# Attention: third score unit behind the mix, next batch's normalising on ScalarE, three engines' orders changed

## The reference

```
xn = (x - mean(x)) / sqrt(var(x) + 1e-5)
q, k, v = xn @ Wq + bq, xn @ Wk + bk, xn @ Wv + bv      # 16 heads of 64
q, k = rope(q), rope(k)
p = softmax(causal(q @ k.T / 8))
x = x + (p @ v) @ Wo + bo
```

## Time and profile before

| | us |
|---|---|
| median of 3 runs | 2759.45 |
| profiled execution | 2767.62 |
| its span | 2765.8 |
| PE busy | 2537.4 (92%) |
| PEld busy | 1909.4 (69%) |
| DVE busy | 1835.4 (66%) |
| ACT busy | 1512.0 (55%) |
| POOL busy | 1462.2 (53%) |

### The profile page before, as it was taken

How to read it: one execution, slowest core, us unless ns; L and a number is a source line. 1 busy time by engine, 2 the same in 40 slices (tenths; PEclk the granted TensorE clock), 3 DMA queues, 4 the chain that set the end, 5 groups by cost and what they waited for, 6 DMA issues and landing times. The chain is left out here.

```text
span 2765.8 us, 53186 instructions
## 1 busy us (share of the span) xinstructions
PE 2537.4 (92%) x16856; PEld 1909.4 (69%) x16856; DVE 1835.4 (66%) x3300; ACT 1512.0 (55%) x3793; POOL 1462.2 (53%) x1264
## 2 busy tenths in 40 slices
PE   7986998899999999999999998999999997986899
PEld 5752676677777777777777776777777774753576
DVE  6741576677777776677767776777677775751376
ACT  2321443666666667666676666766767662321343
POOL 1100543767667677676676766767767661100343
PEclk9997999999999999999999999999999999998999
DMA  7459553323333333233333332323333326359543
GB/s 239 161 226 401 188 156 116 69 58 82 67 71 86 63 71 74 67 84 65 74 81 60 83 65 66 88 64 73 71 71 83 66 63 203 122 203 412 178 151 104
DMA packets 252348, 326.69 MB, mean 118 GB/s; under 512 B 60704, under 2 KB 205728, under 8 KB 247968
## 3 DMA queue, kind: packets, MB, share of 16 engines
q1 hardware_dynamic: 252064, 323.24, 41.5%
HBM read 211.98 MB, written 44.04 MB: 93 GB/s over the span
## 5 line engine op out<-in xcount | busy, mean ns | idle before, releaser
L1524 ACT ACTIVATE att_prob<-att_ps_s,att_nmax 128x512 f32<-128x512 f32 (+3 forms) x1024 | 529.2, 526 | 375.3 <-DVE att_nmax L1426 364.0
L1327 POOL TENSOR_TENSOR att_z_sb<-att_z_sb,sh_vT 128x512 f32<-128x512 f32 x255 | 331.0, 1298 | 381.0 <-DMA att_zs<-att_z_sb 380.9
L1652 PE MATMUL att_ps_p<-sh_ident,att_prob 128*128 128x128 f32 x2560 | 405.5, 282 | 77.9 <-DVE att_probT L1440 76.2
L1426 DVE TENSOR_REDUCE att_nmax<-att_ps_s 128x2 f32<-128x1024 f32 (+3 forms) x512 | 410.2, 822 | 13.3
L1652 PEld LDWEIGHTS att_ps_p<-sh_ident,att_prob 128*128 128x128 f32 x2560 | 296.0, 142 | 132.8 <-DVE att_probT L1440 97.4
L1330 POOL TENSOR_TENSOR att_z_sb<-att_z_sb,att_zs 128x512 f32<-128x512 f32 x255 | 347.0, 1361 | 20.0
L1452 DVE TENSOR_TENSOR att_oT_lo<-sh_kT,att_oT_hi 128x512 fp32r<-128x512 f32 x128 | 158.2, 1236 | 292.0 <-ACT att_oT_hi L1544 292.0
L1328 POOL TENSOR_TENSOR att_zs<-att_zs,att_sin 128x512 f32<-128x512 f32 x255 | 338.0, 1326 | 0.0
L1663 PE MATMUL att_ps_p<-att_probT,att_v_sb 128*64 128x512 f32 (+3 forms) x2048 | 307.1, 442 | 3.7 <-ACT att_probT L1539 2.4
L1539 ACT COPY att_probT<-att_ps_p 128x512 f32<-128x512 f32 x384 | 215.9, 600 | 135.1 <-PE att_ps_p L1652 134.8
L1663 PEld LDWEIGHTS att_ps_p<-att_probT,att_v_sb 128*64 128x64 f32 x2048 | 138.4, 137 | 176.6 <-issue 131.3
(11 more groups left out here) (198 smaller groups left out, 5715.8 us busy)
## 6 DMA issues: line engine op xcount, KB each, us to landing
att_zs<-att_z_sb SPq DMA_DIRECT2D x1024, 64.0 KB, 2.3
ffn_w<-in_e_W SPq DMA_DIRECT2D x56, 1024.0 KB, 13.7
att_R<-inverse_sums SPq DMA_DIRECT2D x256, 128.0 KB, 3.3
ffn_wg<-in_e_Wg SPq DMA_DIRECT2D x24, 1024.0 KB, 14.3
x_normalised_transposed<-dis_b_xnT SPq DMA_DIRECT2D x32, 512.0 KB, 2.7
dis_b_x<-in_x SPq DMA_DIRECT2D x16, 512.0 KB, 4.3
ex_w<-in_e_W SPq DMA_DIRECT2D x8, 1024.0 KB, 12.3
ex_wg<-in_e_Wg SPq DMA_DIRECT2D x8, 1024.0 KB, 15.7
```

The costliest lines, as they stand in the source:

```text
L1327: nc.gpsimd.tensor_tensor(z[:, m, i, :], z[:, m, i, :], cos[:], ALU.mult)
L1426: nc.vector.tensor_reduce(nmax[:, p % 2, qt, :], ps[:, :, at:at + (qt + 1) * P], AX.X, ALU.max, negate=True)\
L1524: nc.scalar.activation(prob[:, p % 2, hh, PLACE[qt]], ps[:, hh, at:at + (qt + 1) * P], ACT.Exp, bias=nmax[:, p % 2, qt, hh:hh + 1], accum_ ...
L1652: last = nc.tensor.transpose(turn_bank(k)[:, at:at + P], prob[:, p % 2, hh, PLACE[qt]][:, kb * P:(kb + 1) * P], g.ident[:])
```

## The change

TensorE: `scores(j, p, 2)` moves from behind the first half of the values to right behind the mix, ahead of both projections. VectorE: the third `largest` moves ahead of `low_part` and the first copy, all four statistics go behind the query's low part, and `normalise` is gone; one small instruction `recentre` makes -mean * rstd. ScalarE: `normalise` is four activations with a scale and a bias for each partition, behind the query copy; `high_part` goes ahead of the evacuations, and the exponentials of tiles 1 and 0 go up, tile 1 between the evacuation of the queries and that of the keys. GpSimd: the rstd of the next batch are made in slot 5 between the rotation of the keys and that of the queries, instead of at the end of slot 4. The code of SP is not changed.

```diff
@@ gpsimd, slot
                     rotate(j, p + 1, 1)
+                    if p == X_TURN and not t.last:
+                        layernorm_rstd(nc, g, pool, mv, veps, rstd, TT, mom_s, veps_s, rstd_s, j + 1)
...
-                if p == X_LOAD and not t.last:
-                    layernorm_rstd(nc, g, pool, mv, veps, rstd, TT, mom_s, veps_s, rstd_s, j + 1)
@@ vector
-            def normalise(j):
+            def recentre(j):
                 dve.wait_ge(rstd_s.sem, rstd_s.at(j, 1))
-                for i in range(TT):
-                    nc.vector.scalar_tensor_tensor(xin[:, i, :], xin[:, i, :], mv[:, i, 0:1], rstd[:, i:i + 1].broadcast_to([P, D]),
-                                                   ALU.subtract, ALU.mult).then_inc(xn_s.sem, 1)
+                nc.vector.scalar_tensor_tensor(shift[:], mv[:, :, 0], -1.0, rstd[:], ALU.mult, ALU.mult).then_inc(stats_s.sem, 1)
@@ vector, slot
-                if loading:
-                    statistics(j + 1, (0, 1))
...
-                if loading:
-                    statistics(j + 1, (2, 3))
+                if p == X_LOAD and not t.last:
+                    statistics(j + 1, range(TT))
                     moments(j + 1)
@@ scalar
+            def normalise(j):
+                act.wait_ge(stats_s.sem, stats_s.at(j, TT + 1))
+                for i in range(TT):
+                    nc.scalar.activation(xin[:, i, :], xin[:, i, :], ACT.Identity, bias=shift[:, i:i + 1], scale=rstd[:, i:i + 1]).then_inc(xn_s.sem, 1)
@@ scalar, slot
                     exps(j, p, 3)
-                if t.has(p):
                     exps(j, p, 2)
+                if t.has(p - 2):
+                    high_part(j, p - 2)
                 if t.has(p + 2):
                     evacuate(j, p + 2, 0)
+                if t.has(p):
+                    exps(j, p, 1)
+                if t.has(p + 2):
                     evacuate(j, p + 2, 1)
@@ tensor, slot
                     mix(j, p - 2)
+                if t.has(p):
+                    scores(j, p, 2)
                 if t.has(p + 2):
                     project(t, p + 2, 0)
```

More of the change, by code:

```diff
@@ L1169, in attention_phase @@
     x_in, xres_in, out_s = c("x_in", 16), c("xres_in", 16), c("out", 16, 16)
-    stats_s, mom_s, veps_s, rstd_s, xn_s = c("stats", TT), c("moments", TT), c("veps", 1), c("rstd", 1), c("xn", TT)
+    stats_s, mom_s, veps_s, rstd_s, xn_s = c("stats", TT + 1, -1), c("moments", TT), c("veps", 1), c("rstd", 1), c("xn", TT)
     xt_mm, xhi_s, xlo_s = c("xt_mm", DC), c("xhi", DC), c("xlo", DC)
@@ L1236, in attention_phase @@
         acc, xout = (sb(x, [P, TT, D]) for x in ("acc", "xout"))
-        stats, mv, veps, rstd = sb("st", [P, TT, 6]), sb("mv", [P, TT, 2]), sb("ve", [P, TT]), sb("rs", [P, TT])
+        stats, mv, veps, rstd, shift = sb("st", [P, TT, 6]), sb("mv", [P, TT, 2]), sb("ve", [P, TT]), sb("rs", [P, TT]), sb("shift", [P, TT])
         xT = g.xT
@@ L1456, in slot @@
                 j, p = t.j, t.p
-                loading, turning = p == X_LOAD and not t.last, p == X_TURN and not t.last
                 if p == X_TURN + 1 and not t.last:
@@ L1467, in slot @@
                     divide(j, p - 2)
-                if turning:
-                    normalise(j + 1)
+                if t.has(p):
+                    largest(j, p, 2)
                 if t.has(p - 2):
@@ L1473, in slot @@
                     copy_pt(j, p - 1, 1)
-                if loading:
-                    statistics(j + 1, (0, 1))
-                if t.has(p):
-                    largest(j, p, 2)
+                if p == X_TURN and not t.last:
+                    recentre(j + 1)
                 if t.has(p - 1):
@@ L1551, in slot @@
                     exps(j, p, 3)
-                if t.has(p):
                     exps(j, p, 2)
+                if t.has(p - 2):
+                    high_part(j, p - 2)
                 if t.has(p + 2):
                     evacuate(j, p + 2, 0)
+                if t.has(p):
+                    exps(j, p, 1)
+                if t.has(p + 2):
                     evacuate(j, p + 2, 1)
-                if t.has(p - 2):
-                    high_part(j, p - 2)
                 if t.has(p + 1):
                     high(j, p + 1, 1)
+                if t.has(p):
+                    exps(j, p, 0)
                 if t.has(p - 1):
@@ L1566, in slot @@
                     high(j, p + 1, 0)
-                if t.has(p):
-                    exps(j, p, 1)
-                    exps(j, p, 0)
+                if p == X_TURN and not t.last:
+                    normalise(j + 1)
                 for u in t.values()[1:]:
@@ L1699, in slot @@
                     values(t, u, 0)
-                if t.has(p):
-                    scores(j, p, 2)
                 if turned:
```

## The result

The changed kernel takes 2816.58 us (median of 4 runs, 2810.78 to 2819.97) against 2758.15 for the kernel before, now of 4 runs: ratio 1.0214, with a 95% interval of 1.0184 to 1.0244. It is 2.1% slower. The forecast was 2785 us, 0.9% slower, with a range of 2735 to 2822. The sign, the mechanism and the range hold; the forecast step is less than half of the measured one.

A forecast was written before the change was run, and what follows sets the result against it. TensorE, 95% busy, was taken to set the pace. A batch of 83.6 + 17.3 + 13.0 = 113.9 against 112.64 us gave +19, with +6 outside +25: 2767.62 became 2792.6, less 8.2 to the median 2785; range 2735 to 2822.

The forecast's parts named there:

- Six plain slots: Attention slots of a batch other than p = 5 and the one after: 13.93 us each, 83.6 together, before 79.6.
- turn slot: Slot p = 5 of each batch: 17.3 us at full clock instead of 20.70, a gain of 3.4.
- what lies outside the 15 batches: First slot and five slots of the last batch: four at +1.1 and about 1 more, together +6 us.
- The ring: Key evacuation, swap and spread DMAs through SP, division, maxima, exponentials, next key evacuation: 13.93 us, once per slot.
- the new wait: TensorE waits 0.5 us in every slot for both first exponentials to free the third score unit's bank.
- step 1: Part of the ring from end of key evacuation to start of VectorE's division: 9.95 us, between 9.4 and 10.50.
- step 2: Part of the ring from VectorE's division through maxima and tile 1 exponentials to end of key evacuation: 3.98 us.
- the third rival: Clock still falls in the turn slot: 3.1 us x 15 = +46 on the forecast, 2831; chance 0.07.
- Slot 6: Slot after p = 5: 11.64 busy + 0.35 + 1.0 wait ahead of the third unit = 13.0 us, before 12.33.
- The step to the median: Takes 8.2 us, the profiled execution's distance above its median, off 2792.6, giving 2785.
- Normalising: Four ScalarE activations replace 5.52 us on VectorE: taken at 1.6 us, hidden, barely, before TensorE asks for the copies.
- First rival: Rows land 9.4 us after key evacuation, the ring is 13.4, TensorE binds at 13.35: 2733 us, chance 0.25.

The follow-up runs named there:

- norm_only: Kernel before, with only the normalising moved from VectorE to four ScalarE activations behind the query copy: 2698.96 us, ratio 0.9775.
- unit_only: Kernel before, with only TensorE's third score unit moved to right behind the mix: 2864.74 us, ratio 1.0386.
- spread_first: Changed kernel, with SP issuing the spread DMAs ahead of the eight swap DMAs: 2751.15 us, ratio 0.9966 to the kernel before.
- both_first: Changed kernel, with SP's spread ahead of the swap and ScalarE's key evacuation ahead of the exponentials of tile 1: 2786.07 us, ratio 1.0081 to the kernel before.

## Why the prediction was right in kind and less than half in size

The steps that failed are in the sum. Its largest mis-sized term is "Six plain slots: 6 x 13.93 = 83.6", which measured 84.48: it was set against a batch average of 112.64 that holds stalls of TensorE which 13.93 leaves out. Its last step carries the distance of one execution from its median over to the other kernel. The turn slot (17.3, measured 17.61) and what lies outside the 15 batches (+6, measured +12) were too small as well. The ring, the new wait and the path through SP were right. In the profiled executions the step was 2815.2 - 2765.8 = +49.4 us of span; the forecast was +25. By its own terms:

- **The ring.** Right. Over the plain slots step 1, taken at 9.95, measured 10.05 on average and step 2, taken at 3.98, 3.99; without the two batches of the next point it is 9.93 + 3.99 = 13.92, for 13.93 forecast. That the middle of two readings of 9.4 and 10.5 hit the mean so closely is luck. The experiments that cut and lengthen the ring bear it out.
- **The wait ahead of the third unit: 0.5 forecast, 0.45 measured in plain slots.** The working was off and the result not: 4.18 + 0.2 - 3.75 is 0.63, and the 0.2 for weights isn't there. The unit starts 0.04 us behind the release in all 126 such waits.
- **Six plain slots: 83.6 forecast, 84.48 measured, +13 us in all.** This is the largest mis-sized term of the sum. In two of 15 batches TensorE stands still for 2.4 to 3.3 us at the end of a plain slot, with nothing that the profile shows to wait for, in the kernel before and after alike; before, then after:

```profile
1107.19 0.50 PE L1638 MATMUL att_ps_s<-att_kT_hi,att_qT_hi 64*128 64x512 f32 x2 [3.30 <-issue]
```

```profile
1127.30 0.80 PE L1641 MATMUL att_ps_s<-att_kT_hi,att_qT_hi 64*128 64x512 f32 x2 [2.43 <-issue]
```

The plain slots of these two batches together take 12.2 us more than those of two average batches of the other 13; in the kernel before it is 7.4. In the other 13 a plain slot takes 13.95, so that about 1 us of the 13 is the ring and 12 are these batches. The 112.64 contained their 7.4 and the 13.93 did not; the other 5 are what the changed kernel loses more in them. What the stalls are is open.
- **Turn slot: 17.3 forecast, 17.61 measured, +5.** At clock 1.00 the mean of eleven is 17.3. Four have a clock of 0.91 and last 18.4: the third rival, at 0.07, came true in four batches of 15, at 1.1 us each and not 3.1. That the eleven hit 17.3 is in part luck: the wait ahead of the third unit was taken at 1.9 in every turn slot and is 1.60 on average (1.95 at most), and a wait of 0.35 for the value copy, taken as hidden, comes on top.
- **Slot 6: 13.0 forecast, 13.03 measured.** Right, term by term: busy 11.70 for 11.64, the wait ahead of the third unit 0.97 for 1.0, and 0.35 for VectorE's copy, where half the old wait was only assumed.
- **Outside the 15 batches: +6 forecast, +12 measured.** The second mis-sized term. The very first slot went from 11.32 to 15.43 us, +4.1, where I had counted it like any other. It is 11.5 in norm_only, 13.8 in unit_only, 14.2 in spread_first and 16.4 in both_first, so it comes with the early unit and needs no ring. What follows the 15 batches is 6.6 longer, what stands ahead of the first slot 1.5.
- **The step to the median.** The 8.2 us by which the profiled execution lay above its median were taken off. The changed kernel's profiled execution took 2816.98 and lies on its median, so that the medians are 58 apart and the spans 49. A gap between one execution and a median is chance and can't be carried over; 2792.6 would have been the forecast without it.

13 + 5 + 6 make the 24 that the span is over the forecast; the rest of the 31.6 us from 2785 to 2816.58 is this last step. No term had a wrong sign. All misses pointed up: stalls, clock falls and the ends of the stage were each left out of a sum that was built from undisturbed slots.

- **Normalising.** Taken at 1.6 us from exponentials; it is 2.08 from the start of the first to the end of the fourth. ScalarE in norm_only:

```profile
567.86 2.08 ACT L1506 ACTIVATE sh_x<-sh_x,att_shift,att_rs 128x256 f32<-128x256 f32 x4
```

The Trainium skill (ScalarE: Activation LUTs, What ACT_TABLE_LOAD costs) adds 93 ns for each pointer operand and gave an estimated 2.0 for the four. The trace agrees, with 2.08. The exponentials were the worse guide: an exponential has one such pointer (`att_nmax`) and lasts 0.47, these have two and last 0.59 each. "Hidden, barely" is nearly right in the changed kernel: TensorE waits for the value copy behind it in 7 turn slots, 5.2 us in all, and 13.1 us in norm_only.
- **First rival (short ring, 0.25).** Wrong, though single passes are as short as it says: in the shortest the rows land 9.38 behind the evacuation. But the mean is 9.94, and a ring takes the mean. "TensorE binds" at 13.35 wasn't reached in spread_first either (13.48).

## What to carry to other kernels

Before an instruction is put ahead of another in a static order, follow what it waits for through every engine and DMA queue until nothing is left, or until you are back at the one you moved: here a delay in the closed ring was paid in full and once per plain slot, while the same delay off the ring cost about a tenth. The cheapest place to cut it was an engine that computes nothing. When a forecast is built from undisturbed slots, compare it with the undisturbed slots of the kernel before, not with an average that holds its stalls. And where a change has several parts, run each alone: here one was worth 60 us and the others hid it.

## What the hardware showed beyond what was expected

The clock doesn't follow the length of a single wait. In the kernel before TensorE idles for 3.2 to 3.3 us at the same place of all 15 turn slots; two of these slots are at 1.00, four at 0.92 and nine at 0.84. In the changed kernel the wait ahead of the third unit is 1.1 to 1.95 us there, and four slots fall, with waits of 1.62, 1.63, 1.78 and 1.92, while the one with 1.95 stays at 1.00. The wait of one that fell, then granted clocks by 3 us windows around it:

```profile
1262.66 0.39 PE L1641 MATMUL att_ps_s<-att_kT_hi,att_qT_hi 64*128 64x256 f32 x2 [1.92 <-ACT att_prob L1524]
```

```profile
1260.00:1263.00 3.00, 1.08 (x14) 0.69 (x12) 2.79 (x6) 1.51 (x5) 2.48 (x2) 1.00 0.30 87
1263.00:1266.00 3.00, 3.00 (x18) 2.30 (x15) 2.85 (x5) 1.67 (x5) 2.85 (x4) 0.57 0.05 11
1266.00:1269.00 3.00, 3.00 (x17) 2.53 (x16) 0.49 (x2) 2.39 (x7) 2.92 (x3) 0.86 0.00 0
1269.00:1272.00 3.00, 3.00 (x28) 3.00 (x27) 1.94 (x4) 3.00 (x9) 2.10 (x2) 1.00 0.40 68
```

It is at half clock (1.2 GHz) for most of the 3 us behind the wait. The turn slot from 1487.78 (above), with a wait of 1.64, stayed at full clock. The slots that fell are 18.4 - 17.3 = 1.1 us longer here, and the one at 0.84 in the earlier trace rows is 3.1 longer than the one at 1.00. Why some slots fall and others with the same wait don't was not settled; no run was made for it.

The delay that a wait for a landed DMA adds to the queue was underrated too: about 1.9 us, where 1.45 were expected.
